# First image of a convolution pair through two transfer queues, weights through GpSimd's, and part of the first chunk's high parts on VectorE

## The reference

```python
# layer 0: depthwise 3x3, then three 64x64 channel mixes (two of them softmaxed)
x = x + _L0_conv_ref(_gn(x), depthwise, pointwise, attention, global_attention)
# layer 1: full 3x3 convolution of sign(x) with sign(w), scaled by mean |w|
x = x + _L1_conv_ref(_gn(x), L1_conv_w)
```

## Time and profile before

| | before |
|---|---|
| median of 3 runs | 1886.92 us |
| the profiled execution | 1885.17 us, of which the span is 1883.3 us (1.9 us lie around it) |
| PE busy | 1768.4 us (94%) |
| DVE busy | 1600.8 us (85%) |
| ACT busy | 1336.3 us (71%) |
| POOL busy | 574.0 us (30%) |

### The profile page before, as it was taken

The page is one execution under the profiler, slowest core; times in us unless marked ns, Lnnn a source line. Parts: engine busy times, 40 slices in busy tenths (PEclk is TensorE's granted clock), DMA queues, the critical chain, the costliest instruction groups (busy, mean ns, idle before and its releaser), DMA issues.

```text
span 1883.3 us, 76437 instructions
## 1 busy us (share of the span) xinstructions
PE 1768.4 (94%) x33132; PEld 1506.3 (80%) x33132; DVE 1600.8 (85%) x2634; ACT 1336.3 (71%) x1463; POOL 574.0 (30%) x341
## 2 busy tenths in 40 slices
PE   0089999999999999999999999999999999999997
PEld 0079777899988877889988888789998788888996
DVE  5668889888898889988899888988899888877776
ACT  2067776777777777777777777777777777677774
POOL 0033332333333333323333333333333333233331
PEclk9999999999999999999999999999999999999999
DMA  9925665565565665555655666556655666432334
GB/s 204 220 72 147 167 153 140 166 152 154 146 156 158 157 154 145 150 156 152 154 144 159 157 156 156 137 158 156 156 145 147 164 152 154 104 89 69 78 78 102
DMA packets 279264, 271.39 MB, mean 144 GB/s; under 512 B 16576, under 2 KB 278848, under 8 KB 279104
## 3 DMA queue, kind: packets, MB, share of 16 engines
q1 hardware_dynamic: 279104, 269.23, 56.2%
HBM read 134.95 MB, written 134.22 MB: 143 GB/s over the span
## 4 chain that ended last, share of the span: by engine, by line
PE 85%; DVE 7%; SPq 4%; issue 2%; ACT 1%; DMA 1%; DVEq 0%; ACTq 0%
PE psA L499 73%; PE psB L499 12%; SPq L260 3%; DVE bnt L720 1%; ACT xh L376 1%; DVE ring L920 1%; DVE ring L886 1%; DMA ring<-in_x 1%; DVE psL L916 1%; DVE pk L897 1%; DVE aggr L827 1%; DVE xc L878 1%; ACT xn L372 0%; SPq L267 0%; DVE sums L731 0%
## 5 line engine op out<-in xcount | busy, mean ns | idle before, releaser
L499 PE MATMUL psA<-xh,W 64*64 64x512 f16 x17912 | 1549.2, 373 | 16.5 <-ACT xh L376 11.9
L499 PEld LDWEIGHTS psA<-xh,W 64*64 64x64 f16 x17912 | 1067.0, 106 | 149.4 <-issue 71.5
L499 PE MATMUL psA<-xl,W 64*64 64x512 f16 x9216 | 984.9, 376 | 0.0
L312 POOL TENSOR_TENSOR xl<-xc,xn 128x1024 f16<-128x1024 f32 (+1 forms) x320 | 571.1, 1794 | 1228.7 <-ACT xn L372 1228.7
L499 PEld LDWEIGHTS psA<-xl,W 64*64 64x64 f16 x9216 | 578.3, 107 | 51.6 <-issue 0.6
L499 PE MATMUL psB<-pk,W 64*64 64x512 f16 (+1 forms) x4944 | 604.0, 362 | 2.3 <-DVE pk L897 1.9
L376 ACT ACTIVATE xh<-xc 64x1024 f16<-64x1024 f32 (+2 forms) x624 | 577.0, 942 | 9.3
L372 ACT ACTIVATE xn<-xc 128x1024 f16<-128x1024 f32 (+2 forms) x264 | 272.1, 1034 | 276.5 <-PE psA L499 191.2
L886 DVE SCALAR_TENSOR_TENSOR ring<-psA,columns,ring 128x1024 f32<-128x1024 f32 x256 | 328.2, 1282 | 141.2 <-PE psA L499 140.7
L720 DVE BATCH_NORM_STATS2 bnt<-ring 128x6 f32<-128x512 f32 x512 | 326.8, 680 | 49.2 <-DMA ring<-in_x 48.9
L499 PEld LDWEIGHTS psB<-pk,W 64*64 64x64 f16 x4944 | 298.1, 106 | 64.5 <-issue 51.0
(11 more groups left out here) (90 smaller groups left out, 133.5 us busy)
## 6 DMA issues: line engine op xcount, KB each, us to landing
out_y<-ring SPq DMA_DIRECT2D x512, 256.0 KB, 3.3
ring<-in_x SPq DMA_DIRECT2D x448, 256.0 KB, 4.0
ring<-in_x SPq DMA_DIRECT2D x32, 512.0 KB, 13.9
pk<-in_w1T SPq DMA_DIRECT2D x2, 144.0 KB, 7.8
ring<-in_w1n SPq DMA_DIRECT2D x2, 144.0 KB, 7.6
grp<-in_same_group SPq DMA_DIRECT2D x1, 64.0 KB, 6.1
ring<-in_dw SPq DMA_DIRECT2D x2, 2.2 KB, 5.6
ring<-in_att SPq DMA_DIRECT2D x1, 16.0 KB, 2.1
```

What stands on the lines that cost most here:

```text
L312: ins = nc.gpsimd.tensor_tensor(xl[:, slot:slot + rows, 1:W + 1], xc[:, j:j + rows], xn[:, k:k + rows, 1:W + 1], ALU.subtract)
L499: mm = pe.matmul(bank[out0:out0 + C, c0:c1], weights[src0:src0 + C, :], src[src0:src0 + C, slot:slot + rows, width[0]:width[0] + width[1]] ...
```

## The change

Four things are changed.

1. The first image goes through two queues: SP issues the 16 transfers of the even rows (partitions 0 to 63) and nothing before them, ACT issues the 16 of the odd rows (`load_pieces`), 6 of them ahead of its first computation and the rest in groups of 3, 3, 2 and 2 between its parts of the weight preparation.
2. All 12 weight transfers are issued by POOL, ahead of its first memsets.
3. For the first image DVE takes no column sums by chunk; one sum over the whole edge columns (`edge_columns`) in `stats_parts` replaces 32 of them. DVE's share of the weight preparation stands behind later pieces than before.
4. For chunk 0 of the first image, DVE makes `xn` and the lower half of `xh` (`xh_first`), ACT only the upper half of `xh`. The border correction is its own function (`border_of_group`) and comes, for the first image, after these.

The core of the diff:

```diff
-            for k, (dst, src) in enumerate(weights):
-                sp.dma_start(dst, src).then_inc(w_in, 16)
-                if k % 4 == 3:
-                    load_piece(k // 4)
-            for p in range(len(weights) // 4, NPIECES):
-                load_piece(p)
+            for p in range(NPIECES):
+                lo, hi = p * NPIECE, (p + 1) * NPIECE
+                sp.dma_start(ring[0:64, lo * CE:hi * CE], xv[0, 0, :, lo * G:hi * G, :]).then_inc(piece_in[p], 16)
...
+            for dst, src in weights:
+                nc.gpsimd.dma_start(dst, src).then_inc(w_in, 16)
...
+            def load_pieces(first, end):
+
+                for p in range(first, end):
+                    lo, hi = p * NPIECE, (p + 1) * NPIECE
+                    nc.scalar.dma_start(ring[64:128, lo * CE:hi * CE],
+                                        xv[0, 1, :, lo * G:hi * G, :]).then_inc(piece_in[p], 16)
+
+            load_pieces(0, 6)
...
+                if n == 0:
+
+                    nc.scalar.activation(xh[C:128, 0:G + 1, 1:W + 1], xc[0:C], ACT.Copy).then_inc(xh_rdy, 1)
+                    return
...
+                if isinstance(n, int) and n == 0:
+                    pe.wait_ge(xh_first, 1)
...
-                ins = nc.vector.reduce_sum(colp[:, :, i], here[:, 0:W:W - 1, :], AX.X)
+                ins = None
+                if img > 0:
+                    ins = nc.vector.reduce_sum(colp[:, :, i], edge_columns(at, G), AX.X)
...
-                nc.vector.reduce_sum(sums[:, img % 2, 2:4], colp[:], AX.X)
+                nc.vector.reduce_sum(sums[:, img % 2, 2:4], colp[:] if img > 0 else edge_columns(0, H // 2), AX.X)
...
             normalise(*of(0))
+            dve.wait_ge(xc_rdy, 1)
+            nc.vector.tensor_copy(xn[:, 2 * G - 1:2 * G, 1:W + 1], xc[:, 0:1])
+            nc.vector.tensor_copy(xn[:, 0:G, 1:W + 1], xc[:, 1:G + 1]).then_inc(xn_rdy, 1)
+            nc.vector.tensor_copy(xh[0:C, 0:G + 1, 1:W + 1], xc[C:128]).then_inc(xh_first, 1)
+            border_of_group(0)
+            dve.wait_ge(xh_first, 1)
             normalise(*of(1))
```

More of the change, by code:

```diff
@@ L195, in conv_preact @@
         xh_rdy = sem("xhigh_ready")
+        xh_first = sem("xhigh_first_ready")
         xl_rdy = sem("xlow_ready")
@@ L289, in _ @@
         def _(pool):
+            weights = ((attx[:, 0, :], att), (attx[:, 1, :], gatt), (pwt, pwT), (idt, ident),
+                       (grp[:], same_group), (member[:], members), (dwt[0:C], dw), (dwt[C:128], dw),
+                       (w1t[0:C], w1T), (w1t[C:128], w1T), (w1m[0:C, :], w1n), (w1m[C:128, :], w1n))
+            for dst, src in weights:
+                nc.gpsimd.dma_start(dst, src).then_inc(w_in, 16)
             for edge in (0, PW - 1):
@@ L335, in _ @@
                                      accum_out=small[:, k, 2:3]).then_inc(exps, 1)
+            load_pieces(6, 9)
             act.wait_ge(w_in, 16 * 12)
@@ L347, in _ @@
             ins.then_inc(w_rdy, 1)
+            load_pieces(9, 12)
             act.wait_ge(mt_rdy, 1)
@@ L353, in _ @@
                                                    scale=dwt[p0:p1, 3 * dy + dx:3 * dy + dx + 1])
+                if p0 == 0:
+                    load_pieces(12, 14)
             ins.then_inc(w0_blocks, 1)
@@ L356, in _ @@
             nc.scalar.activation(W0t, W0f, ACT.Abs).then_inc(abs_rdy, 1)
+            load_pieces(14, NPIECES)
             act.wait_ge(scale_rdy, 1)
@@ L722, in bn_tuples, with edge_columns @@
                 return ins
+            def edge_columns(at, rows):
+                return ring[:, at:at + rows * W].rearrange("p (s w) -> p w s", s=rows)[:, 0:W:W - 1, :]
             def take_borders(img, i):
                 at = place(img, i)
-                here = ring[:, at:at + CE].rearrange("p (s w) -> p w s", s=G)
-                ins = nc.vector.reduce_sum(colp[:, :, i], here[:, 0:W:W - 1, :], AX.X)
+                ins = None
+                if img > 0:
+                    ins = nc.vector.reduce_sum(colp[:, :, i], edge_columns(at, G), AX.X)
                 for edge, (p0, p1), lo in ((0, LO, at), (NC - 1, HI, at + CE - W)):
@@ L739, in stats_piece @@
                     at = place(0, i)
-                    bn_tuples(ring[:, at:at + CE], i)
-                    ins = take_borders(0, i)
-                return ins
-            stats_piece(0)
-            stats_piece(1)
+                    ins = bn_tuples(ring[:, at:at + CE], i)
+                    ins = take_borders(0, i) or ins
+                return ins
+            for p in range(4):
+                stats_piece(p)
             dve.wait_ge(w_in, 16 * 12)
@@ L750, in _ @@
                 link(nc.vector.tensor_scalar(small[:, k, 1:2], small[:, k, 0:1], -1.0, None, ALU.mult))
-            stats_piece(2)
+            stats_piece(4)
             dve.wait_ge(exps, 2)
@@ L756, in _ @@
             ins.then_inc(gt_rdy, 1)
-            stats_piece(3)
+            stats_piece(5)
             dve.wait_ge(prep_mm, 1)
@@ L761, in _ @@
             nc.vector.tensor_copy(U2[:, 1, :], psB[0:C, 0, 0:C]).then_inc(u_rdy, 1)
-            stats_piece(4)
+            stats_piece(6)
             dve.wait_ge(prep_mm, 2)
@@ L785, in _ @@
             ins.then_inc(prep_done, 1)
-            stats_piece(5)
-            stats_piece(6)
+            stats_piece(7)
             dve.wait_ge(prep_mm, 4)
             nc.vector.tensor_copy(MG[:], psL[:, 0, 0:2 * C])
+            for p in range(8, 11):
+                stats_piece(p)
             dve.wait_ge(abs_rdy, 1)
             nc.vector.reduce_max(wst[:, 0:1], w0tf, AX.X).then_inc(amax_rdy, 1)
-            stats_piece(7)
+            stats_piece(11)
+            stats_piece(12)
             dve.wait_ge(amax_all, 1)
@@ L800, in _ @@
             nc.vector.tensor_scalar(osc[:], wst[:, 3:4], 1.0 / (WEXP * XSCALE), None, ALU.mult)
-            for p in range(8, NPIECES):
+            for p in range(13, NPIECES):
                 ins = stats_piece(p)
@@ L856, in scale_of_group, with border_of_group @@
                 steps.link(nc.vector.tensor_scalar(rstd0[:], st[:, 11:12], XSCALE, None, ALU.mult))
+            def border_of_group(img):
+                steps = Steps(stats_chain, STATS_STEPS, img, 14)
                 steps.link(nc.vector.scalar_tensor_tensor(out=parts6[:, 0, :], in0=counts[:], scalar=mean0[:, 0:1],
@@ L964, in _ @@
                         scale_of_group(img + 1)
+                        border_of_group(img + 1)
                 if t + 2 < ALL:
```

## The result

The changed kernel takes 1866.97 us, the median of 4 runs (1866.67 to 1867.5), beside 1887.01 us for the kernel before: ratio 0.9895, 95% interval 0.9883 to 0.9907. That is 20.0 us less, where 30 were forecast. The profiled execution has a span of 1865.3 us instead of 1883.3.

What follows compares the result with a forecast made beforehand. PE bounds the steady state, so only its start at 99.26 us, set by the first image's load, matters. Load 27.5 + 0.1 + tail 2.45 = 30 us off 1886.92 gives 1857 us; range 1848 to 1876, chance 0.80.

Steps and rivals of the forecast that it cites:

- moves as a block: Everything behind PE's first product (256 steps and the tail) shifts with that start, 99.26 us before the change.
- Two queues on two halves: First image's load: two halves in flight together reach all ports, lifting the rate above 222 GB/s.
- 326 GB/s: Assumed two-queue load rate, from stores alone, between bounds 222 and 363; makes the load end 27.5 us earlier.
- the transfers serialise all the same: Rival for the load: engines still wait on every packet, about 235 GB/s, 1877.6 us; chance 0.12.
- no higher rate at all: Rival for the load: rate stays 222 GB/s, only the earlier start counts, 1882 us; chance 0.05.
- Enough if the weights are in by 20 us: ACT's pieces 4 and 5 in flight (6.4 us) keep its queue filled while it waits for DVE's piece 3.
- The likeliest rival: Two queues bring 290 to 363 GB/s in the load, 1863 to 1851 us; chance 0.64.
- the case in between: Load at 235 to 290 GB/s, or ACT's queue runs dry, costing up to 10 us; 1864 to 1877, chance 0.12.
- The end of the load: First image's load: start 2.7, transfer 53.7, landing 0.4, so it ends at 56.8 us, 27.5 us earlier.
- the slower rival: Weights through POOL come late and stop DVE behind piece 3; at the upper bound 1928 us; chance 0.03.
- The tail: Last statistics to PE's first product: casts 2.2 plus border correction 0.45 less edge sum 0.2, 2.45 us gained.
- the fast pace: DVE's three casts of chunk 0 at 0.51 ns an element, 1.8 us together; the slower pace, 1 ns, gives 3.1.

Runs made afterwards that it cites:

- the later comparison: The changed kernel unchanged, timed again beside eight ahead on one chip: ratio 0.9909 to the kernel before, median 1868.32 us beside 1885.87.
- eight ahead: Changed kernel with 8 instead of 6 odd-row transfers issued before ACT's first computation: ratio 0.9856 to the kernel before, median 1859.65 us; repeated, 0.9856, 1858.62 us.
- the split cast: Changed kernel with DVE's cast of 5 rows to `xh` made as two, of 4 rows and 1: one run, 1866.35 us.

## Why the prediction was right, and where it was 10 us off

- *What bounds, and "moves as a block": right.* PE started 19.1 us sooner, and the medians moved by 20.0, in the later comparison by 17.6. In the two profiled executions the stretch from PE's first product to the end is 1784.0 us before and 1785.2 after. Over all twelve profiles it lies between 1782.2 and 1786.0, so this 1.1 us is within the scatter of single executions. Both kernels have windows of 10 us in which PE is busy for less than 10.0 (9.59 from 310 to 320 us before, 9.12 from 330 to 340 after), mostly waiting for nothing that the profile shows; the cause stays open.
- *Two queues on two halves: right,* and shown by the runs with one queue and with two queues on one half; whether SBUF's or HBM's side of a half limits, they leave open. The term "326 GB/s" was too low, 347 was measured. The rivals "the transfers serialise all the same" and "no higher rate at all" are refuted.
- *"Enough if the weights are in by 20 us": this step failed.* It covered 6.4 us of ACT's waiting with pieces 4 and 5 in flight, had DVE through piece 3 "at about 20 us", and counted nothing for a transfer's way from its issue to its first packet. DVE was through at 24.3 and released ACT at 25.05, since flow was only 246 and 273 GB/s up to 15 us (measured from 5 to 10 and 10 to 15) and piece 1 was complete at 15.78. DVE did not wait for the weights. By 25.05 pieces 4 and 5 were nearly in, and the transfer issued then had its first packet 6.8 us later, at 31.87. Why it takes so long beside a full queue of SP no run shows.
- *Luck in the range.* The likeliest rival, 1851 to 1863 at 0.64, did not come; the measured time lies in the case in between, 1864 to 1877 at 0.12, which had named this very gap and priced it at up to 10 us.
- *The end of the load: 56.8 forecast, 66.9 measured.* With the gap closed (eight ahead) it was 58.7, 1.9 us late: the slow start and the end at half the rate cost more than the higher rate gave, so the term is near for two errors of opposite sign. The gap was worth 8.2 us, both at the load's end and at PE's start. DVE's waits for the image were 23.4 us where about 8 were forecast, and still 15.4 with eight ahead, 13 of them for pieces 0 and 1.
- *ACT's issue at "0.65 us each when the queue has room": mis-sized.* Six took 11.92 us, two later ones 6.37: the queue was mostly full. It cost nothing, because ACT was waiting anyway, which the run with all 16 ahead shows by taking that cover away.
- *The weight preparation: hidden, right.* Its last step ended at 60.92 + 1.63 = 62.6 instead of 56, and `normalise` came at 76.5.
- *The weights through GpSimd: 12 issues from 1.27 to 7.9 us,* 0.53 us each as a rule; the slower rival did not come near.
- *The tail: 2.45 forecast, 1.6 measured.* The border correction left the chain as forecast. The edge sum took 0.57 us on the timeline, not 0.42. The casts were 0.30, 0.60 and 1.50 on the chain, 2.4 in all instead of 1.8, and the first product followed `xc` by 2.7 us instead of 2.1: the fast pace was right for the two of `xn` and wrong for the one of 5 rows.

## What to carry to other kernels

Where each transfer writes only half of the partitions, as in this kernel, and the load is the bound, look whether the queue holds the halves one after the other, and if so put the halves in two queues. The engine that issues the second queue then needs a count of its own: enough in flight to bridge its longest wait and, beyond it, the time until a new transfer flows (6.5 to 6.8 us here beside a full queue), and no more than it can issue before its next computation is due. Follow both queues through the windows of the rate; a window at the rate of one half is a queue that has run dry.

## What the runs showed of the hardware

- Two queues that write different halves of the partitions moved 347 GB/s, two that write the same half 207, one queue that alternates 220, at busy shares of 1.10, 1.13 and 1.12. The share did not tell them apart. In all of them a half went with every second 1 KB row in HBM.
- A transfer issued into ACT's queue as it ran out, beside a full queue of SP, had its first packet 6.8 us after its issue (25.06 to 31.87), and 6.5 us with the weights on SP (32.44 to 38.94). At the kernel's start it was 1.5 us.
- 512 KB transfers issued into a full queue hold the issuing engine: 16 of them held ACT for 42.5 us.
- A cast on DVE from fp32 to fp16 of 1280 elements in 5 rows took 1.49 us, one of 1024 in 4 rows 0.69, each beside POOL's low part.
- DVE's small border instruction (6 elements) took 1.25 us beside POOL's low part, and 1.91 us after the split cast, where in the earlier trace rows its place took 0.24. Both times it ended with POOL's second instruction (81.15 and 81.14 us; 82.15 and 82.14).
